# Dropping four of 49 taps from the vector path of a deformable convolution and sending their points to the gather path

## The reference, cut to what matters

```python
xp = x @ in_w + in_b                                     # x: (4, 32, 32, 128), group-normalised
x1 = silu(batchnorm(depthwise_conv3x3(x)))
offset = x1 @ off_w + off_b                              # 8 groups x 9 points x (x, y) for each pixel
mask = softmax((x1 @ mask_w + mask_b).reshape(N, H, W, G, P), -1)
samples = bilinear_sample(xpad, base + grid + offset)    # 4 corners for each of the 9 points
out = (samples * mask).sum(points) @ out_w + out_b
x = x + out
t = t + attention(layernorm(t))
t = t + mixture_of_experts(layernorm(t))
```

## Time and profile before

| | us |
|---|---|
| median of 3 runs (741.1 to 745.64) | 741.61 |
| the profiled execution | 745.32 |
| its span | 743.6 |
| DVE busy | 604.1 |
| PE busy | 588.2 |
| ACT busy | 222.1 |
| POOL busy | 225.0 |

### The profile page before, as it was taken

The page is one execution under the profiler, slowest core; times in us unless marked ns, Lnnn a source line. Parts: engine busy times, 40 slices in busy tenths (PEclk is TensorE's granted clock), DMA queues, the critical chain, the costliest instruction groups (busy, mean ns, idle before and its releaser), DMA issues.

```text
span 743.6 us, 10883 instructions
## 1 busy us (share of the span) xinstructions
PE 588.2 (79%) x3336; PEld 433.7 (58%) x3336; DVE 604.1 (81%) x1094; ACT 222.1 (30%) x324; POOL 225.0 (30%) x275
## 2 busy tenths in 40 slices
PE   5982777796787778778877667668999999938995
PEld 3452555565566556556556555436777777734774
DVE  4489899989899999999999999855777766652666
ACT  6140501500502403305106000024444444413331
POOL 6421802872003782006507310020222111125111
PEclk8786998978997998979989779879999999976999
DMA  6047503003003006000000000000000000004111
GB/s 177 29 183 280 168 1 100 3 2 100 1 0 100 3 2 235 14 0 1 2 0 2 1 0 1 1 0 1 1 0 1 1 1 1 1 2 113 29 44 42
DMA packets 25593, 30.52 MB, mean 41 GB/s; under 512 B 5188, under 2 KB 17684, under 8 KB 25556
## 3 DMA queue, kind: packets, MB, share of 16 engines
q1 hardware_dynamic: 24654, 29.77, 12.2%
q0 software_dynamic: 896, 0.23, 0.4%
q10 hardware_dynamic: 6, 0.00, 0.0%
HBM read 24.94 MB, written 5.05 MB: 40 GB/s over the span
## 4 chain that ended last, share of the span: by engine, by line
PE 50%; DVE 24%; issue 11%; DVEq 2%; ACT 1%; POOL 0%; POOLq 0%; ACTq 0%
PE banks L762 12%; DVE prod L1333 10%; PE banks L872 8%; PE pair L852 7%; DVE stencil L1305 5%; PE pair L917 4%; PE pair L716 4%; PE banks L862 4%; PE banks L951 3%; DVE outer L1299 3%; PE banks L778 2%; PE pair L709 2%; DVE hats L1264 2%; DVEq L1333 1%; PE banks L823 1%
## 5 line engine op out<-in xcount | busy, mean ns | idle before, releaser
L762 PE MATMUL banks<-ident,prod 128*128 128x128 f32 x1528 | 232.6, 305 | 111.3 <-DVE prod L1333 101.8
L762 PEld LDWEIGHTS banks<-ident,prod 128*128 128x128 f32 x1528 | 194.0, 157 | 172.5 <-DVE prod L1333 135.3
L1333 DVE TENSOR_TENSOR prod<-shifted,stencil 128x1024 f32 (+1 forms) x224 | 241.0, 1094 | 12.1 <-PE banks L762 10.1
L716 PE MATMUL pair<-xg,dw_diag 128*128 128x512 f32 x144 | 78.2, 646 | 1.2 <-ACT dw_diag L513 1.2
L872 PE MATMUL banks<-shifted 128*128 128x128 f32 x512 | 63.3, 277 | 2.3 <-ACT shifted L625 1.4
L872 PEld LDWEIGHTS banks<-shifted 128*128 128x128 f32 x512 | 60.2, 192 | 8.1 <-issue 6.1
L1096 POOL CAST far_list_i<-far_list 1x8 int32<-1x8 f32 x8 | 1.5, 191 | 208.1 <-DVEq L1319 202.0
L1299 DVE TENSOR_TENSOR outer<-hats 128x800 f32<-128x800 f32 x64 | 63.4, 991 | 0.8
L1123 POOL TENSOR_TENSOR rstd_now<-mv_now,neg_half 128x2 f32<-128x2 f32 x32 | 22.9, 717 | 134.4 <-DVE mv_now L1401 134.4
L1305 DVE TENSOR_TENSOR stencil<-stencil,outer 128x800 f32 (+1 forms) x64 | 63.3, 989 | 0.3
L852 PE MATMUL pair<-shifted 128*128 128x512 f32 x128 | 60.4, 596 | 0.6 <-ACT shifted L608 0.6
(11 more groups left out here) (221 smaller groups left out, 755.8 us busy)
## 6 DMA issues: line engine op xcount, KB each, us to landing
shifted<-padded SPq DMA_DIRECT2D x42, 256.0 KB, 4.0
shifted<-padded SPq DMA_DIRECT2D x14, 640.0 KB, 8.2
res<-in_x_dram SPq DMA_DIRECT2D x4, 512.0 KB, 5.8
padded<-stage SPq DMA_DIRECT2D x4, 512.0 KB, 2.6
stage<-in_L_ffn_W_dram SPq DMA_DIRECT2D x16, 128.0 KB, 2.1
out_dram<-res SPq DMA_DIRECT2D x8, 256.0 KB, 2.3
padded<-stencil SPq DMA_DIRECT2D x2, 228.0 KB, 2.5
got<-padded,cell_now POOLq DMA_INDIRECT x28, 2.8
```

The lines of the kernel that those rows point to most:

```text
L716: mm = pe.matmul(conv_bank.rearrange("c (r a) -> c r a", r=ROWS), dw_diag[:, t, :], src, start=(t == 0), stop=(t == 8))
L762: mm = pe.matmul(acc_of(c, r), prod[:, d % PROD, r * G:(r + 1) * G, :].rearrange("p g c -> p (g c)"), ident[:, :], is_transpose=True, star ...
L1333: ins = ve.tensor_tensor(prod[:, dx:dx + n, :, :], shifted[:, dx:dx + n, bass.ds(((c % HALF) * ROWS + dy) * G, ROWS * G), :], stencil_of[: ...
```

## The change: what it does

- **45 taps.** The four outermost places of the 7x7 window are left out. The window's rows are taken in another order (`ROW_ORDER`), and a chunk has 26 units, 19 double and 7 single.
- **Those corners go by gather.** A column is now flagged too where a sample at a corner of its 3x3 grid has weight on one of the four left-out places (`corners` on DVE, two instructions). `add_point` no longer takes the whole sample: it works out which of the four corners lie within reach and are not outermost, and sets their weight to zero, since they stay in the near path. That is 12 more POOL instructions for each point.
- **Far flags by ACT.** ACT's `Sign` of (offset - 2) and (-offset - 2), two instructions, takes the place of ACT's square, DVE's maximum and comparison, and two DVE instructions on the masks. PE adds codes, corners and signs up in one row of PSUM, six matmuls instead of one, and DVE's list is read from there.
- **Residual.** PE adds `res` in `project` by a product with the identity, and ACT copies the result back; DVE's addition is gone.
- **Places.** `add_fix` stands at tap 28 and `project` at tap 36 of 45 (before 18 and 25 of 49). The last chunk has no joined pairs.

```diff
+ROW_ORDER = (1, 0, 2, 3, 6, 4, 5)
+TAP_AT = [(dy, dx) for dy in ROW_ORDER for dx in range(WIN) if not (dy in (0, WIN - 1) and dx in (0, WIN - 1))]
+NEAR = len(TAP_AT)
+UNIT_AT = [(t, 2 if t + 1 < NEAR and TAP_AT[t + 1] == (dy, dx + 1) else 1)
+           for t, (dy, dx) in enumerate(TAP_AT) if (dx - (dy in (0, WIN - 1))) % 2 == 0]
-AT_SAMPLES, AT_CONV, AT_FAR, AT_PROJECT = 18, 22, 25, 25
+AT_CONV, AT_FAR, AT_SAMPLES, AT_PROJECT = 22, 25, 28, 36
-JOINED_LAST = (8, 10, 12, 14, 16, 18, 20, 22, 24, 25)
+FAR_UNIT = 8192.0
+def freed_by(tap):
+    dx = TAP_AT[tap][1]
+    before = [t for t in range(tap - NEAR, tap) if TAP_AT[t % NEAR][1] == dx]
+    return before[-1] + 1
...
-                sc.activation(far_xy, raw[:, :, 0:2 * GP], ACT.Square).then_inc(square_done, 1)
...
+                for i, sign in enumerate((1.0, -1.0)):
+                    last = sc.activation(signs[:, i, :, :], raw[:, :, 0:2 * GP], ACT.Sign,
+                                         bias=tap_bias[:, TAPS - 1:TAPS], scale=sign)
+                last.then_inc(signs_done, 1)
...
+            def residual(k):
+                sc.wait_ge(conv_out, k + 1)
...
+                sc.activation(to, bank[0][:, :].rearrange("p (n c) -> p n c", n=B), ACT.Copy).then_inc(res1_done, 1)
...
                 prepare(j + 2)
+                count_out(j + 2)
                 copy_out(j)
-                count_out(j + 2)
+                residual(j)
...
-                pe.matmul(pair[1][:, 0:FAR_COLS], ones16[:, :], far[:, :], start=True, stop=True).then_inc(far_mm, 1)
+                pe.matmul(count, ones[0:1, 0:1], far_codes[:, :], start=True, stop=False)
+                pe.matmul(by_corner, far_unit[:, :], at_corner[:, :, :, :], start=False, stop=False)
+                for i in range(4):
+                    mm = pe.matmul(count, far_unit[:, :], signs[:, i // 2, :, (i % 2) * GP:(i % 2 + 1) * GP],
+                                   start=False, stop=(i == 3))
...
+                    mm = pe.matmul(y, ident[:, :], res[:, n * TILES + k, :], start=False, stop=True)
...
-                step(gp.tensor_tensor(frac[:, 0, :], pos[:, :], low[:, :], ALU.subtract), 7, True)
-                step(gp.tensor_scalar(frac[:, 1, :], frac[:, 0, :], 0.5, 1.0, ALU.add, ALU.mult), 8, True)
...
+                step(gp.tensor_tensor(frac[:, 0, :], pos[:, :], low[:, :], ALU.subtract), 7, False)
+                step(gp.tensor_tensor(tap_d[:, 0, :], low[:, :], place_xy, ALU.subtract), 8, False)
+                step(gp.tensor_tensor(tap_d[:, 1, :], low[:, :], place_mid, ALU.subtract), 9, True)
+                step(gp.tensor_scalar(frac[:, 1, :], frac[:, 0, :], 0.5, 1.0, ALU.add, ALU.mult), 10, False)
+                step(gp.tensor_tensor(tap_c[:, :, :, :], side[:, :, :].unsqueeze(1).to_broadcast([P, 2, 2, 2]),
+                                      tap_d[:, :, :].unsqueeze(2).to_broadcast([P, 2, 2, 2]), ALU.add), 11, True)
...
+                step(gp.tensor_tensor(tap_c[:, :, :, :], tap_c[:, :, :, :], tap_c[:, :, :, :], ALU.mult), 13, True)
...
+                step(gp.tensor_scalar(tap_c[:, 0, :, :], tap_c[:, 0, :, :], float(REACH * REACH) + 0.5, None, ALU.is_le),
+                     15, False)
+                step(gp.tensor_scalar(tap_c[:, 1, :, :], tap_c[:, 1, :, :], float(PAD * PAD) - 0.5, None, ALU.is_ge),
+                     16, True)
...
+                step(gp.tensor_scalar(within[:, :, :], within[:, :, :], -1.0, 1.0, ALU.mult, ALU.add), 22, True)
+                step(gp.tensor_tensor(w_now[:, :, :], w_now[:, :, :], within[:, :, :], ALU.mult), 23, True)
                 gp.wait_ge(gathered, 64)
...
-                ve.wait_ge(square_done, k + 1)
-                own(ve.tensor_tensor(off_most[:, :].rearrange("p (r g) -> p r g", r=ROWS), far_xy[:, :, 0:GP],
-                                     far_xy[:, :, GP:], ALU.max))
-                fill(1)
...
-                own(ve.tensor_scalar(far_flags, off_most[:, :], float(REACH) ** 2, None, ALU.is_gt))
-                fill(1)
...
-                own.link(ve.tensor_tensor(far_part, far_flags.rearrange("p (r o) -> p r o", r=ROWS), mf_rows, ALU.mult))
-                own.link(ve.tensor_tensor(mf_rows, mf_rows, far_part, ALU.subtract))
...
+                for kx in range(2):
+                    x0, y0 = (2 * 3 * TAPS + TAPS - 1) * kx, 2 * 3 * TAPS * kx
+                    last = ve.scalar_tensor_tensor(at_corner[:, :, kx, :], at[:, 0, :, x0:x0 + 2 * TAPS + 1:2 * TAPS], 0.0,
+                                                   at[:, 1, :, y0:y0 + 3 * TAPS:2 * TAPS + TAPS - 1], ALU.is_le, ALU.is_lt)
+                last.then_inc(corners_done, 1)
...
-                own.link(ve.scalar_tensor_tensor(far_first, far_counts[:, bass.ds(k % 2, 1), :].rearrange("a s o -> a (s o)"),
-                                                 0.0, far_codes[:, :], ALU.is_gt, ALU.mult))
...
+                ve.max(far_list[:, :], pair[1][0:1, 0:FAR_COLS]).then_inc(listed, 1)
...
-                    ve.wait_ge(prod_free, c * STENCIL + d + n)
+                    ve.wait_ge(prod_free, c * NEAR + max(freed_by(t), freed_by(t + n - 1)) + PROD)
...
-                    if u in joined(c):
-                        own.link(ins)
-                        ins = ve.tensor_tensor(prod[:, dx, :, :], prod[:, dx, :, :], prod[:, dx + 1, :, :], ALU.add)
```

More of the change, by code:

```diff
@@ L84 @@
 GROUP_UNIT = 128
-FAR_CODE = 4096
+FAR_UNIT = 8192.0
+MOST_CODE = int(FAR_UNIT) * (5 * P + 1) - 1
 PAIRS = B * H // ROWS // 2
@@ L93, in first_of @@
 def first_of(unit):
-    return unit // ROW_UNITS * WIN + unit % ROW_UNITS * 2
-def joined(chunk):
-    return JOINED_LAST if isinstance(chunk, int) and chunk == CHUNKS - 1 else ()
+    return UNIT_AT[unit][0]
+def freed_by(tap):
+    dx = TAP_AT[tap][1]
+    before = [t for t in range(tap - NEAR, tap) if TAP_AT[t % NEAR][1] == dx]
+    return before[-1] + 1
 class Own:
@@ L755, in add_up @@
                 for i in range(first, last):
[L756 to L760 removed]
+                    c, t = k + i // NEAR, i % NEAR
+                    slot = TAP_AT[t][1]
+                    pe.wait_ge(prod_done, c * NEAR + t + 1)
                     for r in range(ROWS):
[L762 to L764 removed]
+                        mm = pe.matmul(acc_of(c, r), prod[:, slot, r * G:(r + 1) * G, :].rearrange("p g c -> p (g c)"),
+                                       ident[:, :], is_transpose=True, start=(t == 0 and r == 0), stop=False)
+                    mm.then_inc(prod_free, 1)
             def add_fix(k):
@@ L790, in turn @@
                 offsets(k + 1)
-                add_up(k, first_of(BEGIN), AT_SAMPLES)
-                if not first:
-                    add_fix(k - 1)
-                add_up(k, AT_SAMPLES, AT_CONV)
-                for i in range(AT_CONV, STENCIL):
-                    if i == AT_PROJECT and not first:
-                        project(k - 1)
+                add_up(k, first_of(BEGIN), AT_CONV)
+                for i in range(AT_CONV, NEAR):
                     if conv_ahead and i == AT_CONV:
@@ L803, in turn @@
                         count_far(k + 1)
+                    if i == AT_SAMPLES and not first:
+                        add_fix(k - 1)
+                    if i == AT_PROJECT and not first:
+                        project(k - 1)
                     add_up(k, i, i + 1)
-                add_up(k, STENCIL, STENCIL + first_of(BEGIN))
+                add_up(k, NEAR, NEAR + first_of(BEGIN))
             turn(0, True, True)
@@ L973, in _ @@
             own(gp.memset(ones16[:, :], 1.0))
+            own(gp.memset(far_unit[:, :], FAR_UNIT))
             own(gp.memset(group_mean[:, :], 1.0 / GN_C))
@@ L1000, in _ @@
                 gp.iota(far_codes[:, r * GP:(r + 1) * GP].rearrange("p (g q) -> p g q", g=G),
-                        pattern=[[GROUP_UNIT + PTS, G], [1, PTS]], base=FAR_CODE + r * G * GROUP_UNIT, **whole)
+                        pattern=[[GROUP_UNIT + PTS, G], [1, PTS]], base=int(FAR_UNIT) * 4 * P + r * G * GROUP_UNIT, **whole)
             gp.iota(corner[:, :].rearrange("p (a b) -> p a b", a=2), pattern=[[B * HP * G, 2], [G, 2]], base=0, **whole)
             gp.memset(stride[:, 0:1], float(B * HP * G))
+            for c in range(2):
+                gp.memset(side[:, c, :], c - 0.5)
             own.link(gp.memset(stride[:, 1:2], float(G)))
@@ L1080, in add_point @@
-                w_flat = w_now[:, :, :].rearrange("p a b -> p (a b)")
-                step(gp.tensor_tensor(w_flat, w_flat, off_m.to_broadcast([P, 4]), ALU.mult), 11, True)
+                middle = bass.ds((group % G) * PTS + PTS // 2, 1)
+                place_mid = here[:, bass.ds(row3, 2), middle].rearrange("p a o -> p (a o)")
+                step(gp.tensor_tensor(frac[:, 0, :], pos[:, :], low[:, :], ALU.subtract), 7, False)
+                step(gp.tensor_tensor(tap_d[:, 0, :], low[:, :], place_xy, ALU.subtract), 8, False)
@@ new lines, in add_point @@
+                w_flat = w_now[:, :, :].rearrange("p a b -> p (a b)")
```

(21 more changed lines are left out.)

124 lines of the change are left out of this document (62 added, 62 removed).

## The result

The change made the kernel slower: **779.88 us** (median of 4 runs, 778.2 to 780.52) against 743.62 us for the kernel before (median of 4, 741.1 to 749.17), a ratio of **1.048, interval 1.0436 to 1.0531**. The profiled execution took 779.73 us, with a span of 777.9.

A forecast was written before the change was run, and what follows sets the result against it. POOL's chain of gathered points was taken to set the pace, delaying attention's first statistics from 488.09 to 512.5 us: +24.4 us, so 745.3 becomes 770 profiled, 766 as median. Range 734 to 790 us.

The forecast's parts named there:

- F(k): POOL's chain: the time in us when POOL is through with chunk k, needed at PE's tap 28 of the next turn.
- L(k): DVE's list of far points: the time in us when chunk k's list is there for POOL.
- 11 points, 7 before: POOL's gathers: flagged columns counted per chunk as 1, 3, 2, 2, 0, 1, 2, 0, with 44 gathers expected.
- 0.95 us for a step beside a busy DVE, about 34 us for a point: POOL's points: 12 added steps at 0.95 us add 11.4 us, making about 34 us a point beside a busy DVE.
- DVE's waits of 8 to 20 us in turns 2, 3 and 4, put down to PE: Sign of being right: DVE idles 8 to 20 us in those turns, with PE named as what it waits for.
- A turn of 50.5 us that waits for nothing else: DVE's middle turn: 53.0 us less 1.5, 0.6 and 0.9, plus 0.4 for corners; expected in turns 1, 5 and 6.
- The 4.13 us of the second gather issue: POOL's gather issue before the change, against 0.94 and 1.30 us for others; left unchanged in the sum.
- L(2) = 172: Chunk 2's list on DVE, forecast to be there at 172 us, after chunk 1's at 119.
- The 4.7 us ahead of a chunk's first point: POOL's start of a chunk, 4.7 us before its first point, read from the trace before the change.
- third rival, starvation: Last chunk: gap-free DVE products hold up POOL; chunk 6 loses up to 8 us more; 775 us; chance 0.07.
- the first case: Main forecast: POOL sets the pace at 0.7 to 1.1 us a step; 766 us; chance 0.66.
- The first rival, covered gathers: POOL's added steps cost 0.31 us each, gathers stay covered, kernel faster: 726 us; chance 0.16, fourth rival included.

The follow-up runs named there:

- x1: The changed kernel, but POOL handles no listed point, so gathers and their sums are left out of the result: 724.95 us, ratio 0.976.
- x2: The changed kernel's 11 points with the old 15 POOL steps each, the 12 added steps removed: 737.37 us, ratio 0.989.
- x3: The changed kernel with columns flagged by corner alone left out, so 7 points of 27 steps: 725.27 us, ratio 0.976.
- h1: The changed kernel with all 49 taps, no corner flags, 7 points of 22 steps, two more units before the wait for the hats: 714.99 us, ratio 0.964.
- x4: The changed kernel, but DVE waits for its own list instruction's end in every turn before going on to the products: 759.13 us, ratio 1.025.
- h2: h1 with DVE waiting for its own product behind the third, fourth and fifth product of the last chunk: 711.05 us, ratio 0.958.
- x5: The changed kernel, but in the last chunk DVE waits for each product's end from the third on: 773.06 us, ratio 1.043.

## Why the prediction was right

The forecast was 766 us, slower; it is 779.9, slower, within the range. The mechanism is the one forecast, and x1, x2 and x3 show it from three sides. Point by point, with F(k) read where POOL takes up the next chunk (its CAST) and L(k) at the end of the list's MAX8:

```
                          forecast   measured
F(1), chunk 1 finished    220        218.8
F(2)                      286        283.4
F(3)                      352.5      348.1
L(6), list of chunk 6     418.5      416.2
L(7)                      469        467.3
F(6)                      494        502.3
first statistics          512.5      521.1
```

- **11 points, 7 before**: right, 44 gathers.
- **0.95 us for a step beside a busy DVE, about 34 us for a point**: right, 0.97, and 160.58 - 128.04 = 32.5. Beside a waiting DVE I took 0.31, and it is 0.26.
- **DVE's waits of 8 to 20 us in turns 2, 3 and 4, put down to PE**: right, 12.6 us each.
- **A turn of 50.5 us that waits for nothing else**: 51.7. The wait for the hats is there (2.87; my 4 us less 1.5 gives 2.5). What I left out is the wait for PE's banks at the offsets, 1.28 us, where the kernel before has 0.58. By the kernel's `freed_by`, the unit that waits writes slots 3 and 4, and slot 4 comes free with tap 4, the first that PE adds behind the offsets matmuls. Without the outermost places a row of five columns is paired from column 1, so this is the row's second unit, where with seven columns it was the third. DVE's mask comes late by it, and ACT's exponential waits 1.00 us for the mask (ACT's row at 129.72; no such wait before), with the hats behind it. In h1, with seven columns again, the two waits are 0.57 and 0.31 us.
- **The 4.13 us of the second gather issue**, which I left as it is, are gone: in the first points of chunks 1, 5 and 6 no issue takes over 2.17 us. I had said this would follow if they came from an instruction that the change removes, such as the flags' comparison. DVE's order around them changed too, so the runs don't show which it was.
- **L(2) = 172** was a slip in the sum: it is 53 us after L(1), and my own turn of 50.5 gives 169.5. The end of that list is at 170.4.
- **The 4.7 us ahead of a chunk's first point** was wrong where the list finds POOL idle: 9.2 us (118.85 to 128.04), since the CAST waits 5.6 us for DVE's first gap. I had noted that part of the list goes, and had counted that only as 0.9 us off DVE. The gap that I removed from DVE was POOL's way in, and POOL lost about 5 us at each later list as well (5.79, 5.90 and 5.91 us in turns 2, 3 and 4), which the sum had at nothing. Points whose steps fell into DVE's waits and short instructions were shorter than 34 us and made up for it: the second of chunk 1 took 29.5 (160.58 to 190.11). That F(1) to F(3) came within 1.2 to 4.4 us of the forecast is in part luck; x4 shows that F(1) is 202 with the gap.
- **F(6) and the last chunk**: this is the term that was mis-sized, by 8.3 us. It is my third rival, starvation, with its price ("up to 8 us more") and its cause. I gave it 0.07 as if it excluded the first case. It did not: both happened, POOL's pace and the starvation. I should have put the term into the sum, because the earlier trace rows already showed nine products without a gap where chunk 6's second point would have to be worked.
- **Behind F(6)** the sum had the wrong path, and it was luck that the length fitted. I had POOL work chunk 7 for 12 us and 6.5 us follow. In fact PE adds chunk 7's `stage` at 515.58 without waiting for POOL: from 501.59 on, the taps left to DVE and PE set the pace, and it is 19.5 us to the statistics. Part of this is PE's clock. After its wait of 17.14 us the granted clock is 0.54 of full from 501.5 to 508, so mostly at the lower level (1.2 GHz), and 32 transposes take 6.12 us; from 511.65, at full clock (2.4 GHz), 36 take 4.09. That is about 2.5 us, where my upper bound had allowed 5 without a row for it.
- **From profile to median**: the sum was 745.3 + 24.4 = 769.7 for the profiled execution, and this took 779.73, 10.0 us more: the 8.6 us to the first statistics and 1.4 behind them. The other 3.9 us of the miss are the step from one profiled execution to the median. I took off 3.7 us, since the one of before was slow for its kernel; the one of after sits at its median.
- **The first rival, covered gathers**: its 726 (710 with nothing from POOL) can now be read. Without any point it is 725, not 710. The first statistics come at 468.2, where that sum had 456, and all of the difference lies in the last chunk: its list is there at 425, as in the sum (456 less 31), because my 53 us for the first turn and a first list 1.6 us earlier nearly make up for the longer turns (51.4 us). From list to statistics x1 takes 43.2 us, and I had 31. POOL's CAST of 23.92 us makes up about 8 of these 12: PE waits 5.4 us for POOL, and at a granted clock of 0.50 it is then 8.4 us from PE's `stage` to the statistics, against 5.5 in h2. The other 4 I had too little for the products and the tail. The rest of the 15 us is the 3.7 us that I took off for the median, as above.

What stays open: when POOL gets in between DVE's instructions and when not. It does in the stretch of stencils (0.97 us a step, so about one step for each DVE instruction). Between products alone, which follow each other almost as closely, it mostly does not (18.84, 19.16, 23.92 and the 5.6 us), but in x4 four steps did, and in the kernel before three steps ran from 342.80 to 345.53 beside four products without a gap (341.39 to 345.47). So a run of products without a gap is not by itself enough to shut POOL out. What the runs show is that a wait of DVE for its own instruction's end lets POOL in (x4, x5, h2). How x4's 9.61 and 10.69 us of waiting in turns 3 and 4 arise was not taken apart.

## What to carry to other kernels

A side engine that has slack on the page can be one queue of dependent small steps: count its busy stretch from one handover to the next, not its share, and price added steps by what its neighbour does at that moment. A saving on the bounding engine is worth nothing in front of a wait; h1 did two more units in a shorter turn. And before closing the last gap of an engine, look for who lives in it: 0.3 to 0.6 us given back behind the list instruction of each turn took 17 us off the kernel.

## What the runs showed of the hardware

- **POOL can be shut out for many DVE instructions in a row, not for one.** A CAST of 8 numbers took 0.18 us with a gap of 0.25 us (x4) or 0.44 us (the kernel before) on DVE, 5.60 us beside six gap-free DVE instructions, and 23.92 us beside 24. An addition of 16 numbers a partition took 19.16 us beside 19 (x2). Each ended within 0.1 us of the end of DVE's run. It is no rule for every such run: the four steps of x4 from 458.23 on got in, and the CAST at 469.51, beside the same run, did not.
- **It holds for the issue of an indirect DMA as well**, 18.84 us beside 19 plain products. The Trainium skill, "SBUF — State Buffer", section "Who interferes with whom", says that `tensor_tensor` with two inputs in SBUF holds up GpSimd's reads, which the steps of 0.97 us agree with. It also infers that `tensor_tensor` spares the generation of descriptors. The row at 468.17 speaks against the inference, or else a read of the cell numbers ahead of the descriptors was held up; the runs don't tell which.
- **Breaking such a run is cheap**: with a wait of DVE on its own result behind each product, a product costs 1.20 us instead of 1.00, and with such waits from the third product on h2's CAST is through in 3.27 us.
